# Wide attention on one core: who scales the experts' rows, and in how many operations they are added to the residual

## The reference

```
logits = x_norm @ router_w.T + router_b
topv, topi = top_k(logits, 2);  gates = softmax(topv)
for e in experts:
    w = sum(gates * (topi == e))
    out += w * ((silu(x_norm @ gate_w[e].T) * (x_norm @ up_w[e].T)) @ down_w[e].T)
x = x + out                                   # the residual after the mixture
x = x + wide_attention(layernorm(x), Wq, Wk, Wv, Wo, bo)
```

## Time and profile before

| | |
|---|---|
| median of 3 runs | 1297.98 us |
| the profiled execution, its own time | 1297.34 us |
| its span, first to last instruction | 1295.5 us |
| PE, DVE, ACT, POOL busy, share of the span | 80%, 69%, 42%, 42% |
| wide attention, first gather to last addition | 675.4 to 1086.6 us |
| of it the steady blocks 1 to 13, by PE's starts | 730.6 to 1043.1 us |

### The profile page before, as it was taken

How to read it: one execution, slowest core, us unless ns; L and a number is a source line. 1 busy time by engine, 2 the same in 40 slices (tenths; PEclk the granted TensorE clock), 3 DMA queues, 4 the chain that set the end, 5 groups by cost and what they waited for, 6 DMA issues and landing times. The chain is left out here.

```text
span 1295.5 us, 39531 instructions
## 1 busy us (share of the span) xinstructions
PE 1035.7 (80%) x14827; PEld 838.1 (65%) x14828; DVE 892.4 (69%) x2134; ACT 548.0 (42%) x877; POOL 549.5 (42%) x686
## 2 busy tenths in 40 slices
PE   2999968999935779999975999999999994661453
PEld 1566654666634679999974888888888884441112
DVE  1778764878643934444426999999999986337787
ACT  1556634666511046666632444444444442110343
POOL 3323314434220033333315888888888773103000
PEclk9999976999955579999996999999999998555555
DMA  3000000000061011111121000000000001110002
GB/s 87 2 3 0 2 24 19 18 9 9 2 228 40 0 33 49 47 47 48 46 73 45 16 11 13 10 11 11 10 12 10 9 0 35 47 52 17 1 0 65
DMA packets 33367, 37.54 MB, mean 29 GB/s; under 512 B 6344, under 2 KB 26507, under 8 KB 32908
## 3 DMA queue, kind: packets, MB, share of 16 engines
q1 hardware_dynamic: 28942, 27.64, 6.9%
q0 software_dynamic: 4352, 8.92, 2.7%
HBM read 27.63 MB, written 8.91 MB: 28 GB/s over the span
## 5 line engine op out<-in xcount | busy, mean ns | idle before, releaser
L1167 POOL DMA_INDIRECT e_x<-xn_rows,e_where x72 | 68.5, 951 | 202.8 <-DVE e_where L1148 116.9
L1137 DVE COPY e_y<-e_Y_ps 128x128 f32<-128x128 f32 x72 | 21.0, 291 | 109.3 <-PE e_Y_ps L1104 109.3
L1324 POOL TENSOR_TENSOR a_E<-a_E,a_rsum 128x512 f32<-128x512 f32 x64 | 66.7, 1042 | 50.7 <-DVE a_rsum L1688 50.7
L262 POOL TENSOR_SCALAR a_KX<-a_KT,a_of_head 128x512 f32<-128x512 f32 x64 | 43.0, 696 | 85.7 <-ACT a_KT L454 85.7
L1094 PE MATMUL e_G_ps<-e_xT,e_gate_here 128*128 128x128 f32 x576 | 77.9, 279 | 0.5 <-ACT e_up_here L1057 0.5
L1094 PE MATMUL e_U_ps<-e_xT,e_up_here 128*128 128x128 f32 x576 | 77.1, 277 | 0.0
L262 POOL TENSOR_SCALAR x_KX<-x_KT,x_of_head 128x512 f32<-128x512 f32 x64 | 43.1, 698 | 78.8 <-issue 49.9
L1104 PE MATMUL e_Y_ps<-m_down_w,e_hT 128*128 x576 | 76.0, 275 | 0.2 <-DVE e_hT L1155 0.2
L1056 ACT ACTIVATE e_gate_here<-m_gate_w 128x512 f32 x72 | 45.4, 630 | 70.7 <-PEq L85 44.9
L1094 PEld LDWEIGHTS e_G_ps<-e_xT,e_gate_here 128*128 128x128 f32 x576 | 71.7, 196 | 0.7 <-ACT e_up_here L1057 0.7
L1094 PEld LDWEIGHTS e_U_ps<-e_xT,e_up_here 128*128 128x128 f32 x576 | 71.2, 194 | 0.0
(11 more groups left out here) (302 smaller groups left out, 2838.9 us busy)
## 6 DMA issues: line engine op xcount, KB each, us to landing
slot_out<-e_y SPq DMA_DIRECT2D x72, 64.0 KB
x_ctxT<-in_ctxT SPq DMA_DIRECT2D x16, 256.0 KB
m_gate_w<-in_L_ffn_gate_w SPq DMA_DIRECT2D x1, 2048.0 KB
m_up_w<-in_L_ffn_up_w SPq DMA_DIRECT2D x1, 2048.0 KB
m_down_w<-in_L_ffn_down_w SPq DMA_DIRECT2D x1, 2048.0 KB
xn_rows<-r_xn SPq DMA_DIRECT2D x8, 256.0 KB
x_ctxK<-in_ctxK SPq DMA_DIRECT2D x8, 256.0 KB
out_x<-q_y SPq DMA_DIRECT2D x8, 256.0 KB, 2.2
```

Source lines behind the costliest of these rows:

```text
L262: last = nc.gpsimd.tensor_scalar(KX[:, p, :, h * T:(h + 1) * T], src, of_head[:, h:h + 1], 1.0, ALU.mult, ALU.mult)
L1167: nc.gpsimd.indirect_dma_start(out=x[:, j, :], out_offset=None, in_=k.xn_rows, in_offset=bass.IndirectOffsetOnAxis(ap=where[:, j, :], axis ...
L1324: nc.gpsimd.tensor_tensor(e, e, rsum[:, g % 2, :].unsqueeze(2).broadcast_to([P, GH * UB, T]), ALU.mult)\
```

## The change

ScalarE multiplies the rows of each expert by their gates, into two new planes beside the residual: `k.XR` is `[128, 3, 32, 128]`, plane 0 is the old `k.X`, and `apply_gates` writes planes 1 and 2. It is called at the end of g = 0 (experts 0) and of g = 1 (experts 1), for the block two ahead, two activations of 128 x 128 a time. VectorE's `combine` is one `tensor_reduce` a block, which reads the three planes with the plane as innermost index and writes 256 sums per partition to a new tile `X_of_second_layer`, which is `k.X` from here on. It is called at the end of g = 2, directly ahead of `statistics`. The gathers wait for `gated` (ScalarE's count) where they waited for `combined`.

```
+            def apply_gates(nb, i, p):
+                act.wait_ge(got[p][i], (nb // 2 + 1) * (16 * UB))
+                for u in range(UB):
+                    rows = k.XR[:, 1 + i, bass.ds(nb * UB + u, 1), :].rearrange("p o c -> p (o c)")
+                    last = nc.scalar.activation(rows, expert_rows[:, p, i, u, :], ACT.Copy, scale=k.gates[:, i, bass.ds(nb * UB + u, 1)])
+                last.then_inc(gated, 1)
...
             def prologue():
                 slots_of(0, 0)
                 slots_of(1, 1)
+                for i in range(2):
+                    apply_gates(0, i, 0)
+                for i in range(2):
+                    apply_gates(1, i, 1)
                 normalise(0)
...
                     evacuate_o(blk, g)
+                    if later(nxt, 2) and g < 2:
+                        apply_gates(blk + 2, g, p)
...
-            def combine(nb, i, p):
-
-                if i == 1:
-                    wait_here(dve, combined, nb * 2 + 1, passed)
-                dve.wait_ge(got[p][i], (nb // 2 + 1) * (16 * UB))
-                for u in range(UB):
-                    x = k.X[:, nb * UB + u, :]
-                    last = nc.vector.scalar_tensor_tensor(out=x, in0=expert_rows[:, p, i, u, :],
-                                                          scalar=k.gates[:, i, bass.ds(nb * UB + u, 1)], in1=x,
-                                                          op0=ALU.mult, op1=ALU.add)
-                last.then_inc(combined, 1)
+            def combine(nb):
+
+                wait_here(dve, gated, nb * 2 + 2, passed)
+                rows = k.XR[:, :, bass.ds(nb * UB, UB), :].rearrange("p i u c -> p (u c) i")
+                nc.vector.tensor_reduce(k.X[:, bass.ds(nb * UB, UB), :].rearrange("p u c -> p (u c)"), rows, AX.X, ALU.add)\
+                    .then_inc(combined, 1)
 
             def statistics(nb):
-                wait_here(dve, combined, nb * 2 + 2, passed)
+                wait_here(dve, combined, nb + 1, passed)
...
                     if later(nxt, 2):
-                        if g in (0, 1):
-                            combine(blk + 2, g, p)
+                        if g == 2:
+                            combine(blk + 2)
                         if g == 2:
                             statistics(blk + 2)
```

More of the change, by code:

```diff
@@ L1239, in wide_attention_phase @@
         got = [[sem(f"got{p}{i}") for i in range(2)] for p in range(2)]
+        gated = sem("gated")
         combined = sem("combined")
@@ L1337, in gather @@
                     if later(nb, 2):
-                        pool.wait_ge(combined, (nb - 1) * 2)
+                        pool.wait_ge(gated, (nb - 1) * 2)
                     wait_here(pool, where_ready, nb + 1, passed)
@@ L1697, in prologue @@
             def prologue():
-                for i in range(2):
-                    combine(0, i, 0)
+                combine(0)
                 statistics(0)
@@ L1706, in prologue @@
                 products_k(0, 1)
-                for i in range(2):
-                    combine(1, i, 1)
+                combine(1)
                 statistics(1)
@@ L2386, in sb @@
             return ctx.enter_context(nc.sbuf_tensor(name, shape, dt))
-        k.X = sb("X", [P, NU, C])
+        k.XR = sb("XR", [P, 3, NU, C])
+        k.X = k.XR[:, 0]
+        X_of_second_layer = sb("X_of_second_layer", [P, NU, C])
         k.ident = sb("ident", [P, P])
@@ L2404, in decoder_kernel @@
         mixture_phases(nc, k)
+        k.X = X_of_second_layer
         run_phase(nc, wide_attention_phase, k)
```

## The result

The kernel after took 1304.08 us in the median of 5 runs (1301.72 to 1306.27), the kernel before 1298.95 us (1297.2 to 1300.1, 5 runs beside it). The ratio is 1.0040, with a 95% interval of 1.0023 to 1.0057: slower by 5.1 us, where 5.1 us faster was forecast. The time lies in the stated range, on the other side of no change, and near the 1305.7 of the slow planes. Their mechanism was not there, though: the reduction took 1.02 us. The profiled execution took 1301.72 us (span 1299.7).

A forecast was written before the change was run, and what follows sets the result against it. VectorE was taken to set the pace, with TensorE close behind. Loop -5.8, lump in block 0 +0.5 and prologue +0.2 gave -5.1 us, from 1297.98 to 1292.9 us; range of 8 in 10: 1288.5 to 1306.5.

The forecast's parts named there:

- the slow planes: Rival: reads 16 KB apart cost a second nanosecond per input, reduction 1.90 us, block 24.39, kernel 1305.7 us; chance 0.33.
- TensorE alone: TensorE's own block is 23.14 us; as rival, a shorter lump leaves no item waiting, kernel 1286.8 us; chance 0.07.
- The rule of the item: TensorE's item lasts the longer of 5.65 us and D + 3.49 us, plus 0.31 at the loop's turn (g = 3).
- D: VectorE's lateness: start of its row maximum after the start of TensorE's item; 1.17 us at least, 2.61 forecast at g = 3.
- ScalarE's pair: Two gating activations, 0.88 us, in ScalarE's 1.00 us idle gap before the exponentials' copy; costed at nothing.
- the lump at g = 2: VectorE's step at g = 2: 4.67 own work, 1.10 reduction, 1.32 statistics, 7.09 us, making the g = 3 item 6.41 us.
- The expected gain: In the loop, a block falls from 24.02 to 23.59 us, 0.43 us less.
- theory M: From the experiments: VectorE enters at a rotation's end if GpSimd's chain began from a stall, else at chain's end; 0.5 us in e15.
- Theory P: From the experiments: VectorE enters early only if the last k product still runs as the first q rotation begins; 1.85 us in e15.

The follow-up runs named there:

- e2: Kernel after with both gating pairs at the end of g = 0 and the reduction at the end of g = 1: 1286.98 us, ratio 0.9921.
- e7: e2 with the variances written as a reduction, as in e1: 1281.07 us, ratio 0.9908.
- e4: Kernel after, its reduction reading 768 neighbouring numbers instead of three planes (wrong sums): 1300.62 us, one run.
- e1: Kernel after with the variances as a reduction over the variance and a stored EPS instead of tensor_scalar: 1292.06 us, ratio 0.9956.
- e14: e2 with three small memsets on GpSimd ahead of the softmax's multiplication at the end of g = 2: 1302.62 us, one run.
- e15: Kernel after with GpSimd's softmax multiplication at the end of g = 2 also waiting for the k products: 1290.23 us, one run.
- e3: Kernel after without the reduction, the experts never added: 1299.75 us, one run.
- e17: e3 with GpSimd's bias added at the end of g = 2 instead of g = 1: 1303.91 us, one run.
- e8 to e13: Kernel after or e3 with small reductions ahead of the variances, bn_stats on one row, or GpSimd's k rotation waiting longer: 1295.54 to 1304.73 us, one run each.
- e16: e2 with GpSimd's softmax multiplication at the end of g = 2 also waiting for the k products: 1287.83 us, one run.

## Why the prediction was wrong

**Right.** VectorE set the pace before: with less work on it (e2, e7) the block falls to 23.17 or 23.18 us, near the 23.14 put for TensorE alone. The reduction costs 1.18 us from start to start, forecast 1.10, bounds 0.95 to 1.25; the planes are nearly free (e4). The rule of the item, D + 3.49 + 0.31, holds in the kernel after: VectorE enters g = 3 at 824.97 - 821.75 = 3.22, which gives 7.02 for the 7.07 read. D at g = 2 is 817.27 - 816.10 = 1.17, as said. ScalarE's pair ends at 811.87, and the copy of the exponentials waits another 0.33 us for TensorE:

```profile
811.19 0.68 ACT L1580 ACTIVATE XR<-a_expert_rows,gates 128x128 f32 x2
812.21 0.60 ACT L1566 ACTIVATE a_ET<-a_KE_ps 128x512 f32<-128x512 f32 x1 [0.33 <-PE a_KE_ps L1454]
```

An activation takes 0.39 us in the mean (put at 0.44). The centres are unchanged (0.72 us). In the prologue the statistics of block 0 start at 686.15 (forecast 686.3).

**The step that failed** is the lump at g = 2, "4.67 + 1.10 + 1.32 = 7.09". Its terms measured 4.74, 1.18 and 1.78, together 7.70. The last was carried over from the kernel before as a constant, and with it the 467 ns of the variances. It is mostly a wait for GpSimd, and its length depends on where GpSimd's chain stands, which the change moves. The other terms are 0.15 us above theirs. The trace of before could have told: in its loop the variances end at 823.15, and a rotation of GpSimd's ends at 823.12 (822.40 + 0.72), while in its prologue, with no rotation beside them, they take a third of the time:

```profile
685.93 0.17 DVE L1636 TENSOR_SCALAR a_var_eps<-a_mv 128x2 f32<-128x2 f32 x1
```

With 7.70, D at g = 3 is 3.22 instead of 2.61, the item 7.07 instead of 6.41, and with 0.14 more at g = 0 (6.02 us for the 5.88 read in block 14) the block is 24.39 instead of 23.59. e1 shows it: with that one instruction in a form that does not wait for GpSimd, the lump is 6.93, the block 23.62 and the time 1292.06 us; the kernel after was put at 1292.9. That e1 comes so near is in part luck: its variances take 0.3 us less than the forecast's, its reduction, the work ahead of it and its item at g = 0 together 0.3 us more.

**Over the phase.** In the kernel before, blocks 1 to 13 last from 730.6 to 1043.1 us, 312.5 us; in the kernel after from 731.13 to 1047.87:

```profile
731.13 0.31 PE L1437 MATMUL a_S_ps<-causal_keys,causal_queries 64*64 64x128 bf16 x8
1047.87 0.31 PE L1437 MATMUL a_S_ps<-causal_keys,causal_queries 64*64 64x128 bf16 x8 [0.18 <-issue]
```

That is 316.7 us, 4.3 more, and with the 0.5 by which block 1 starts later 4.8 us. The two profiled executions differ by 4.4 us (1301.72 and 1297.34), the medians by 5.1, so the loop has the whole loss.

**The rivals.** The slow planes gave 24.39 us a block and 1305.7 us, the block to the hundredth and the time nearly, by a mechanism that took next to no part (0.08 of the 0.80 us). Had the runs stopped at the total, it would have passed for the cause. For TensorE alone the prediction named the right row, the variances beside GpSimd's work, but let it move in one direction: "0.3 us less at their new place". It moved by 0.44 the other way. The stated criterion, a block over 23.8 us, caught the error.

**Why GpSimd is late now.** At the end of g = 1 GpSimd has the bias besides its other work: from one multiplication to the next, without a stall, 5.63 us. In the kernel before VectorE's reciprocals came 6.18 us apart there (814.25 to 820.43), since two combining instructions stood between them, and GpSimd stood still for 0.40 us ahead of the multiplication at 820.72. Without them they come 5.38 us apart (815.33 to 820.71), and GpSimd goes from work to work:

```profile
815.62 1.04 POOL L1325 TENSOR_TENSOR a_E<-a_E,a_rsum 128x512 f32<-128x512 f32 x1 [1.09 <-DVE a_rsum L1697]
820.57 0.74 POOL L1331 TENSOR_TENSOR X_of_second_layer<-X_of_second_layer,a_bias_row 128x256 f32 x1
821.25 1.05 POOL L1325 TENSOR_TENSOR a_E<-a_E,a_rsum 128x512 f32<-128x512 f32 x1
824.31 0.71 POOL L1305 TENSOR_TENSOR a_RK<-a_PK 128x256 f32<-128x256 f32 x1
```

Reciprocals that come 0.8 us sooner there took GpSimd's pause, and with the pause, by e14 and e15, the place where VectorE is let in. The expected gain, 0.43 us a block, was more than given back (24.39 us against 24.02), and 0.46 of the 0.80 us between forecast and measurement went into a wait that nobody had edited.

The sign to look for is the distance from the reciprocals' start to the multiplication's: 0.28 or 0.29 us where GpSimd waits for them (814.25 to 814.53 and 820.43 to 820.72 in the kernel before, 817.46 to 817.74 in e2, where no gap is to be seen), 0.54 in the kernel after (820.71 to 821.25). One run has both cases. In e3 the distance is 0.28 us in the loop's first block and 0.53 to 0.56 in the twelve that follow, and the variances are short in the first (725.36) and long in the twelve (748.29 is the first of them):

```profile
725.36 0.52 DVE L1641 TENSOR_SCALAR a_var_eps<-a_mv 128x2 f32<-128x2 f32 x1
748.29 2.14 DVE L1641 TENSOR_SCALAR a_var_eps<-a_mv 128x2 f32<-128x2 f32 x1
```

**What stays open.** That the time at which GpSimd's chain starts turns one case into the other is shown both ways (e14; e15 and e17), and the later signals and the distance to a boundary are ruled out as the cause (e8 to e13). Whether it is a late start, one that follows work without a pause (theory M), is not shown, and two sets of rows speak against it. In e16 the centres are let in though the multiplication beside them (817.63) followed the power without a gap:

```profile
818.00 0.72 DVE L1655 SCALAR_TENSOR_TENSOR a_centre<-a_mv,a_rstd 128x2 f32<-128x2 f32 x1
```

And in e14 one block has its multiplication 0.36 us behind the reciprocals, straight behind the memsets, and its variances (725.74) are let in after 0.59 us; in the twelve blocks at 0.38 and 0.39 they wait out the chain. Over all runs, some 600 such instructions that VectorE issued ahead of the third rotation's end, the distance alone separates the cases: let in at 0.28 to 0.36, at 0.93 to 0.95 (e16's centres) and at 1.45 to 1.47 us, not at 0.38 to 0.62. The first rotation begins 1.00 us behind the multiplication, and VectorE's last k product ends 1.39 us behind the reciprocals (822.10 in the kernel after). So the long cases are those in which that rotation begins at the end of this product or within some 0.25 us behind it. Theory P had a bound on one side only, and e15 and e16 refute it in that form; a window with two sides fits every row, and no run was made to tell it from theory M, nor one between 0.62 and 0.93 us. Why either should let VectorE in is open too.

## What to carry to other kernels

A duration read from a busy loop can be a wait in disguise: where a small instruction takes several times what it takes at its least (0.17 us for these variances with no rotation beside them), don't carry it to another place as a constant; ask which instruction of the other engine it ends with. Beside a busy GpSimd, a small addition was better written in a form that isn't held up: as a reduction it took 157 ns in every block of e1. And work taken from one engine can take pauses from its neighbours: before counting it as a gain, look whether the neighbour was pausing there.

## What the hardware showed unexpectedly

- A VectorE instruction on 128x2 numbers lasted 0.17, 0.32, 0.50, 0.94, 1.11, 1.66, 1.94, 1.99, 2.04 or 2.16 us, by where GpSimd's chain stood, and a scalar_tensor_tensor on the same size 0.72 or 3.10 us. In the long cases its end lies within 0.04 us of the end of GpSimd's last rotation, over up to four ends of GpSimd's instructions on the way. The Trainium skill, SBUF — State Buffer, section "Who interferes with whom", has the shared pair held "for the whole instruction"; by that rule the wait would end with the GpSimd instruction that it began beside, and in the long cases it doesn't.
- A reduction over groups of three costs what the groups of 8 and 64 gave: 944 ns for 768 neighbouring inputs, where 1.00 ns an input from the earlier trace rows gives 931. Over planes 16 KB apart it takes 1024 ns. The Trainium skill, Advanced Engine Details and Errata, section SBUF Cachelines, would have each of these inputs penalised; the measured penalty is 0.08 us, 0.1 ns an input.
- A wait that an engine has no need of (e15) can make a block shorter than the same one without it: 23.95 for 24.39 us.
